# A two-layer Perceiver block on one core: pairs counted while the router runs, stage openings reordered

## The chip, the cores and the metric

The program runs on one core of a Trainium2 chip. The metric is the time of one execution on the device in microseconds (us); less is better. A core has five engines that work side by side and wait for each other through semaphores: TensorE (PE, matrix products; its weight loads are PEld), VectorE (DVE), ScalarE (ACT), GpSimd (POOL) and SyncE (SP, which here only issues transfers).

## What is computed

x is (128 sequences, 32 tokens, 256 numbers), ctx is (128, 257, 256). Every step is added to x; LN is a layer norm without weights.

```python
x0: x += Wo(softmax(q(LN x) . k(ctx) / 4) v(ctx))        # cross-attention, 16 heads of 16, Wq Wk Wv Wo
s0: x += softmax(q(LN x) . k(LN x) / 4) v(LN x)          # self-attention over the 32 tokens
moe: xf = LN(x).reshape(4096, 256)
     routing = softmax(xf @ router_w.T)                  # 8 experts
     top_w, top_i = top_k(routing, 2); top_w /= sum(top_w)
     x += sum over the 2 of top_w * (w_down[e] @ (silu(w_gate[e] @ xf) * (w_up[e] @ xf)))
x1: x += Wo(softmax(q(LN x) . k(ctx) / 4) v(ctx))        # one matrix Wq for q, k and v
s1: x += W_out(causal softmax(rope(q) . rope(k) / 8) v)  # 16 heads of 64, W_qkv is 256 x 3072
bit: x += BitLinear(LN x)
```

## The kernel before

The 4096 tokens are 32 slices (G) of 128 rows; four slices (GPS) make a group, so there are 8 groups (SG). x stays in SBUF as X (128 partitions x 32 slices x 256). The program is five stages, one after the other, each a block with one hand-written list of instructions for each engine: CrossAttention "x0", SelfAndRouter ("s0" and the router, tiles named _moe), Experts ("moe"), CrossAttention "x1", SelfAttention1 ("s1" and "bit"). An engine works through its list in order. Between two stages all five engines meet at a barrier, so nothing of the next stage is issued before the last engine is done with this one.

**s0 and the router.** A loop over g runs one slice of self-attention per step; j is g modulo 4, i is g divided by 4. Group i+1 is prepared in the shadow of group i: its rows are turned at j=0 and projected to q, k, v at j=1, 2, 3 (`project`). The router trails by two groups: at j=0 PE turns the rows of group i-2 (`router.turn`), at j=1 it makes the logits, and DVE makes at j=2 in `choose` some 20 small instructions whose last writes `both`, the table of which 2 of 8 experts each token takes. PE's results go through a ring of only two PSUM banks; who takes a bank waits until it has been emptied (`banks.take(name, signal)`). The loop has 7 steps more than slices, in which the last two groups are routed. SP issues in it the loads of the experts' weights (1.5 MB an expert: 3 experts early, 5 at g=35, `E_FIRST`), the stores of each group's rows (`leave_rows`), and at the end waits for the last of these stores.

**Experts.** 71 tiles of 128 token-expert pairs. First a plan: PE multiplies `both` with a triangle of ones and with ones (`count`), DVE makes running sums over the 32 slices (`scan`), each pair's tile and row (`row`), the experts of the tiles (`plan_experts`), then codes in four pieces (`code`), which PE multiplies; DVE decodes them to token numbers and POOL fetches the rows of a tile with an indirect transfer. SP loads the high halves of the gate and up weights (2 x 4 MB, `fetch_hi`) after the barrier. PE's first product waits for them and for the first tile's rows.

**x1.** A loop over 128 sequences i (j is i modulo 16, a group has 16); DVE takes the maxima of a step's scores (L764), turns v (L780) and the probabilities (L788). At j=5 to 9 the next group of x is normed and turned, at j=12 and 13 projected to q. Before the loop DVE adds the experts' results to group 0 (L844), then norms it. SP keeps one queue of transfers: weights, ctx (1 MB for four sequences), X and y (1.5 MB for a group), and in each step v out to HBM and back to `v_wide`. A load of ctx waits until ctx two groups back has been split into high and low halves.

**s1.** Group 0 is normed (DVE, POOL), turned (PE) and split; the weights Wq, Wk, Wv (1 MB each) are loaded and split by ACT (high) and DVE (low); then slices follow.

A product in high and low halves is three fp32r products (`split_product`, L230). The lines that the steps of the change touch:

```python
sp.wait_ge(self.s.s_pv, "s0", G - 1)           # SelfAndRouter.sync, at g >= G
for e in range(E_FIRST, E):
    self.gates.fetch(sp, self.w.tile, e)
...
dve.wait_ge(self.s.s_x0, i * GPS + GPS - 1)    # take_rows: all four slices
...
for w in (*self.wqkv, self.wout):              # SelfAttention1.sync
    w.load(sp)
```

## Time and profile before

| | us |
|---|---|
| median of 3 runs (2652.72 to 2662.46) | 2653.41 |
| the profiled execution | 2663.03 |
| its span (first to last instruction) | 2661.2 |
| PE busy in the span | 2435.1 (92%) |
| DVE busy | 1827.3 (69%) |
| ACT busy | 1231.6 (46%) |
| POOL busy | 839.3 (32%) |
| mean granted TensorE clock | 0.957 |

The profiled execution is 1.8 us longer than its span and 9.6 us longer than the median of the runs. Busy shares are means over stages that have different limits: in the middle of a stage an engine is nearly full, at the four seams between stages PE is idle or at half clock. The granted clock is a share of full speed: 1.00 is 2.4 GHz, 0.50 is 1.2 GHz.

### The profile page before, as it was taken

The page shows a single profiled execution, that of the slowest core. Times are in us where ns is not written, and L with a number is a line of the kernel's source. Part 1 is how long each engine was busy: PE and PEld are TensorE (multiplying, and loading weights), DVE is VectorE, ACT ScalarE, POOL GpSimd, SP SyncE. Part 2 cuts the span into 40 slices and gives each one's busy share as a digit, 9 for nine tenths or more (in the row PEclk, how much of TensorE's full clock was granted, in tenths as well). Part 3 has the DMA queues.
Part 4 walks back from the last instruction along what each step waited for, and adds up shares of the span by engine and source line. Part 5 has one row for each costly group of instructions (what it writes and reads, how often), then busy time and mean ns, then how long its engine had stood idle before and what let it go on. Part 6 is the DMA issues. An engine that isn't in the chain of part 4 may idle for free. (4 is left out here: it accounts for less than half of the span.)

```text
span 2661.2 us, 102781 instructions
## 1 busy us (share of the span) xinstructions
PE 2435.1 (92%) x44604; PEld 1996.7 (75%) x44604; DVE 1827.3 (69%) x3898; ACT 1231.6 (46%) x2732; POOL 839.3 (32%) x728
## 2 busy tenths in 40 slices
PE   7999999999978846999995989888997999999997
PEld 6888888888845535888884767767775888888885
DVE  5677677767657664222225888888887888888886
ACT  5666565666535423333324666556664322323322
POOL 3233333332222112433335333343321332332331
PEclk9999999999989867999998999999998999999998
DMA  6444555553313253111116776767674000000000
...
DMA packets 171903, 298.94 MB, mean 112 GB/s; under 512 B 26296, under 2 KB 104252, under 8 KB 161984
## 3 DMA queue, kind: packets, MB, share of 16 engines
...
## 5 line engine op out<-in xcount | busy, mean ns | idle before, releaser
L900 POOL TENSOR_TENSOR ctxT_x_lo<-ctx_in_x,ctxT_x_hi 128x514 fp32r<-128x514 f32 x256 | 307.6, 1202 | 757.0 <-ACT ctxT_x_hi L700 757.0
L721 ACT ACTIVATE prob_x<-ps_score_x,neg_max_x 128x257 f32<-128x257 f32 x1024 | 403.5, 480 | 246.3 <-DVE neg_max_x L764 246.3
L764 DVE TENSOR_REDUCE neg_max_x<-ps_score_x 128x2 f32<-128x514 f32 x512 | 328.7, 683 | 99.3 <-PE ps_score_x L611 98.9
L622 PEld LDWEIGHTS ps_v_x<-v_wide_x,probT_x 128*32 128x32 f32 x18432 | 293.9, 110 | 103.2 <-issue 75.3
L622 PE MATMUL ps_v_x<-v_wide_x,probT_x 128*32 128x68 f32 x18432 | 340.5, 226 | 31.5 <-issue 21.6
L788 DVE STREAM_TRANSPOSE probT_x<-prob_x 128x1152 f32<-128x1152 f32 x256 | 345.9, 1351 | 0.0
L2240 POOL TENSOR_TENSOR rot_s<-turned_s,swapped_s 128x512 f32<-128x512 f32 x128 | 164.4, 1297 | 300.5 <-DVE swapped_s L2164 260.4
L611 PE MATMUL ps_score_x<-kT_x,q_x 32*64 32x257 f32 x4096 | 179.4, 406 | 24.6 <-ACT prob_x L721 21.8
L712 ACT ACTIVATE kT_x<-ps_x,bias_k 128x257 f32<-128x257 f32 x256 | 122.1, 477 | 165.1 <-PE ps_x L230 165.1
L1776 DVE TENSOR_TENSOR hid_moe<-ps_up_moe,silu_moe 128x512 f32<-128x512 f32 x71 | 49.1, 692 | 203.0 <-PE ps_up_moe L230 203.0
L230 PE MATMUL ps_x<-ctxT_x_hi,w_q_x_hi 128*128 128x258 f32 x512 | 163.6, 319 | 15.2 <-POOL ctxT_x_lo L900 15.2
L230 PE MATMUL ps_x<-ctxT_x_hi,w_v_x_hi 128*128 128x258 f32 x512 | 160.1, 313 | 12.8 <-POOL ctxT_x_lo L900 11.6
L230 PE MATMUL ps_s<-w_qkv_s_hi,xT_s_hi 128*128 128x512 f32 x384 | 164.4, 428 | 5.5 <-ACT w_qkv_s_hi L264 2.8
L700 ACT ACTIVATE ctxT_x_hi<-ctx_in_x 128x514 fp32r<-128x514 f32 x256 | 161.7, 632 | 6.8 <-DMA ctx_in_x<-ctx 6.8
L230 PE MATMUL ps_x<-ctxT_x_hi,w_k_x_hi 128*128 128x258 f32 x512 | 158.8, 310 | 1.4 <-DVE v_x L780 1.4
L230 PE MATMUL ps_s<-w_qkv_s_lo,xT_s_hi 128*128 128x512 f32 x384 | 152.5, 397 | 0.0
L230 PE MATMUL ps_s<-w_qkv_s_hi,xT_s_lo 128*128 128x512 f32 x384 | 152.3, 396 | 0.0
L230 PE MATMUL ps_x<-ctxT_x_lo,w_q_x_hi 128*128 128x258 f32 x512 | 149.1, 291 | 2.5 <-issue 2.5
L230 PE MATMUL ps_x<-ctxT_x_hi,w_q_x_lo 128*128 128x258 f32 x512 | 148.9, 291 | 0.0
L2117 ACT ACTIVATE attnT_s_hi<-ps_s 128x512 fp32r<-128x512 f32 x64 | 38.1, 598 | 232.4 <-PE ps_s L2035 232.4
L230 PE MATMUL ps_x<-ctxT_x_lo,w_v_x_hi 128*128 128x258 f32 x512 | 145.4, 284 | 0.0
L230 PE MATMUL ps_x<-ctxT_x_hi,w_k_x_lo 128*128 128x258 f32 x512 | 145.3, 284 | 0.0
...
## 6 DMA issues: line engine op xcount, KB each, us to landing
...
v_wide_x<-v_x SPq DMA_DIRECT2D x512, 76.5 KB, 2.2
v_out_x<-v_x SPq DMA_DIRECT2D x128, 306.0 KB, 3.2
v_wide_x<-v_out_x SPq DMA_DIRECT2D x512, 76.5 KB, 2.6
...
```

The lines of the kernel that those rows point to most:

```text
L230: last = pe.do.matmul(out, a, b, start=n == 0, stop=n == len(steps) - 1)
L611: ins = pe.do.matmul(self.ps[m * 2 * T:(m + 1) * 2 * T, r, 0:S], q, self.kT[b % 3][rows, m, 0:S], start=True, stop=True)
L622: ins = pe.do.matmul(self.ps_v[r * T:(r + 1) * T, b % 2, :, :], self.probT[b % 3][:, r, n * T:(n + 1) * T], self.v_wide[b % 4][:, :, r, n, ...
L700: act.do.activation(self.ctxT[b % 3].hi[:, :, 0:S], self.ctx_in[g % 2][:, :, j, :], ACT.Copy).then_inc(*s.ctx_hi.at(tag, b))
L712: act.do.activation(out, src, ACT.Identity, bias=self.biases["k"][:, m:m + 1]).then_inc(*s.k.at(tag, b, m))
L721: act.do.activation(self.prob[b % 3][:, r, 0:S], self.ps[:, r, 0:S], ACT.Exp, bias=self.neg_max[b % 2][:, r:r + 1]).then_inc(*s.exp.at(tag ...
L764: dve.do.tensor_reduce(self.neg_max[b % 2][:, r], self.ps[:, r, 0:S], AX_X, ALU.max, negate=True).then_inc(*s.neg_max.at(tag, b, half))
L788: dve.do.transpose(flat(self.probT[b % 3]), flat(self.prob[b % 3])).then_inc(*s.prob_T.at(tag, b))
L900: pool.do.tensor_tensor(self.ctxT[b % 3].lo[:, :, 0:S], self.ctx_in[g % 2][:, :, j, :], self.ctxT[b % 3].hi[:, :, 0:S].bitcast(F32), ALU.s ...
L1776: dve.do.tensor_tensor(self.hid[t % 2][:, :], self.up_ps[t % 2][:, :], self.silu[t % 2][:, :], ALU.mult).then_inc(*s.hid.at(t))
L2117: act.do.activation(self.attnT.hi[:, c * 512:(c + 1) * 512], banks["attn", g, c][:, :], ACT.Copy).then_inc(*s.a_hi.at(g, c))
L2240: pool.do.tensor_tensor(self.rot[e][:, :, :], self.turned[e][:, :, :], self.swapped[e][:, :, :], ALU.add).then_inc(*s.r_rot.at(g, i, c))
```

## The change

Four parts.

1. **Counting moves into s0.** The new class Places counts a group's pairs as soon as the group is routed: five bf16 products of 128 x 40 on PE (`count`, at j=3, from the same ring of two banks) and two DVE instructions (`add`). `both` becomes bf16 with five empty slices beside each group's four, so that the five products give running sums. The two big products, the scan of 32 slices and its memsets go from Experts; `plan_experts` moves behind the four codings; the memsets of x_in move from DVE to POOL.
2. **Loads and the last rows.** Experts 5 to 7 are loaded after the last rows have been stored (`E_SECOND`). `take_rows` waits slice by slice; in the last steps ACT scales the last rows before the exponent of the group ahead, not after it.
3. **x1's opening.** X and y of group 0 are loaded first; DVE splits the low half of the weight after it has added y, not before.
4. **s1's opening moves into x1.** Group 0 of x is normed, turned and split during x1's last 16 steps (stats at j=5, 6, scale at 7, halves at 8, 9). Wq is loaded at i=112 and split in steps 126 to 129, into tiles that the ctx halves have left; Wk and Wv are loaded after the last ctx has been split.

```diff
 class Places:
+    def count(self, pe, i, banks):
+        bank, emptied = banks.take(("count", i), self.s.plan, "placed", i)
+        pe.wait_ge(self.s.route, i, ROUTE_STEPS - 1)
+        if emptied:
+            pe.wait_ge(*emptied)
+        out = bank[:, 0:(GPS + 1) * E]
+        for d in range(GPS + 1):
+            ins = pe.do.matmul(out, (self.ones if d else self.below)[:, :],
+                               self.both[:, i, GPS - d:2 * GPS + 1 - d, :].rearrange("p g e -> p (g e)"), start=d == 0, stop=d == GPS)
+        ins.then_inc(*self.s.counted.at(i))
+    def add(self, dve, i, banks):
+        ...
+            dve.do.tensor_tensor(self.place[:, g, :], out[:, 0:GPS, :], self.total[:, i - 1, :].unsqueeze(1).to_broadcast([P, GPS, E]),
+                                 ALU.add)
+            dve.do.tensor_tensor(self.total[:, i, :], out[:, GPS, :], self.total[:, i - 1, :], ALU.add).then_inc(*s.plan.at("placed", i))
 SelfAndRouter.sync:
-                    for e in range(E_FIRST, E):
+                    for e in range(E_FIRST, E_SECOND):
                         self.gates.fetch(sp, self.w.tile, e)
...
+        for e in range(E_SECOND, E):
+            self.gates.fetch(sp, self.w.tile, e)
 SelfAndRouter.tensor:
             if now is not None:
                 a.scores(pe, g)
+            if j == 3 and routed is not None:
+                self.places.count(pe, routed, banks)
...
+        self.places.count(pe, SG - 1, banks)
 SelfAndRouter.scalar:
+            if g == G + 1:
+                router.scale(act, rows)
             if j == 1 and routed is not None:
                 router.exponent(act, routed)
-            if g == G + 1:
-                router.scale(act, rows)
 SelfAndRouter.vector:
         def take_rows(i):
-            dve.wait_ge(self.s.s_x0, i * GPS + GPS - 1)
             for n in range(GPS):
+                dve.wait_ge(self.s.s_x0, i * GPS + n)
                 router.ln.take_stats(dve, i, n)
...
             if now is not None:
                 a.find_max(dve, g)
+            if j == 3 and routed is not None:
+                self.places.add(dve, routed, banks)
 Experts.vector:
         plan()
-        plan_experts()
         dve.wait_ge(s.plan, "row")
         for c in range(2 * G // CHUNK):
             code(c)
+        plan_experts()
 CrossAttention.sync:
+        if self.opening:
+            load_y(0)
         for n in self.of_ctx:
             self.w[n].load(sp)
         load_ctx(0)
...
+            if self.opening and i == B - BPS:
+                sp.wait_ge(s.y_added, SG - 1)
+                self.opening.wq.load(sp)
...
+        if self.opening:
+            sp.wait_ge(s.ctx_hi, tag, B - 1)
+            sp.wait_ge(s.ctx_lo, tag, B - 1)
+            for w in self.opening.wkv:
+                w.load(sp)
 CrossAttention.vector:
+            if self.opening and n == SG:
+                if j in (5, 6):
+                    dve.wait_ge(s.x_out, tag, GPS - 1)
+                    for half in range(GPS // 2):
+                        self.opening.ln.take_stats(dve, 0, (j - 5) * (GPS // 2) + half)
+                if j == 7:
+                    self.opening.ln.scale(dve, 0)
+                if j in (8, 9):
+                    dve.wait_ge(s.q_ps, tag, SG - 1, KD - 1)
+                    self.opening.ln.keep_lo(dve, 0, j - 8, banks)
+            if self.opening and 0 <= i - B < 2:
+                dve.wait_ge(s.k_ps, tag, B - 1, KD - 1)
+                self.opening.wq.split_lo(dve, i - B)
 SelfAttention1.vector:
-        for j in range(GPS):
-            self.ln.take_stats(dve, 0, j)
-        self.ln.scale(dve, 0)
-        self.wqkv[0].split_lo(dve)
-        prepare(0)
         self.wqkv[1].split_lo(dve)
```

What the lists of the engines look like at three places. Names carry the stage (_s0, _moe, _x1, _s1); in brackets are the signals that an instruction waits for.

PE at a step j=3 of s0 before: scores of the slice (q_s0 and kT_s0), then the two halves of v of the next group (w_v_s0), then the weighing of the slice ahead (probT).

```order
L1153 MATMUL ps_score_s0<-kT0_s0,q0_s0_15937 64x32 [waits s_shift]
L1153 MATMUL ps_score_s0<-kT0_s0,q0_s0_15937 64x32 x31
L1114 MATMUL ps_1_s0<-xT1_s0,w_v_s0 128x512 [waits k]
L1114 MATMUL ps_1_s0<-xT1_s0,w_v_s0 128x512
L1114 MATMUL ps_0_s0<-xT1_s0,w_v_s0 128x512 [waits k]
L1114 MATMUL ps_0_s0<-xT1_s0,w_v_s0 128x512
L1193 MATMUL ps_v0_s0<-v_wide0_s0_15941,probT0_s0 32x68 [waits s_out,s_probT]
L1193 MATMUL ps_v0_s0<-v_wide0_s0_15941,probT0_s0 32x68 x15
L1153 MATMUL ps_score_s0<-kT1_s0,q1_s0_15938 64x32 [waits s_shift]
```

And in the change:

```order
L1210 MATMUL ps_score_s0<-kT0_s0,q0_s0_15937 64x32 [waits s_shift]
L1210 MATMUL ps_score_s0<-kT0_s0,q0_s0_15937 64x32 x31
L1403 MATMUL ps_1_s0<-both_routed,below_placed 128x40 [waits k,route]
L1403 MATMUL ps_1_s0<-both_routed,ones_placed 128x40 x4
L1171 MATMUL ps_0_s0<-xT1_s0,w_v_s0 128x512 [waits k]
L1171 MATMUL ps_0_s0<-xT1_s0,w_v_s0 128x512
L1171 MATMUL ps_1_s0<-xT1_s0,w_v_s0 128x512 [waits plan]
L1171 MATMUL ps_1_s0<-xT1_s0,w_v_s0 128x512
L1250 MATMUL ps_v0_s0<-v_wide0_s0_15941,probT0_s0 32x68 [waits s_out,s_probT]
```

The count stands ahead of the v products and waits for the route, which is DVE's `choose`; the second half of v takes the bank of the count, and so waits for "plan", which is DVE's `add` of this step.

PE at the end of s0 and over the barrier before: logits of group 6, turns of the last rows (group 7), its logits, then the two products that count all pairs.

```order
L1263 MATMUL ps_0_s0<-router_moe,xT0_moe 128x8 [waits m_xT]
L1263 MATMUL ps_0_s0<-router_moe,xT0_moe 128x8 x7
L349 MATMUL ps_1_s0<-constants,ln_xn1_moe 128x128 [waits ln_moe_xn]
L349 MATMUL ps_1_s0<-constants,ln_xn1_moe 128x128 x3
L349 MATMUL ps_0_s0<-constants,ln_xn1_moe 128x128 [waits route]
L349 MATMUL ps_0_s0<-constants,ln_xn1_moe 128x128 x3
L1263 MATMUL ps_1_s0<-router_moe,xT1_moe 128x8 [waits m_xT]
L1263 MATMUL ps_1_s0<-router_moe,xT1_moe 128x8 x7
L2282 UNCONDITIONAL_BRANCH
L2283 UNCONDITIONAL_BRANCH [waits barrier_Pool_Activation_PE_DVE_SP_release]
L1535 MATMUL ps_0_moe<-both_routed,constants 128x256 [waits route]
```

And in the change:

```order
L1320 MATMUL ps_0_s0<-router_moe,xT0_moe 128x8 [waits m_xT]
L1320 MATMUL ps_0_s0<-router_moe,xT0_moe 128x8 x7
L1403 MATMUL ps_1_s0<-both_routed,below_placed 128x40 [waits route]
L1403 MATMUL ps_1_s0<-both_routed,ones_placed 128x40 x4
L352 MATMUL ps_0_s0<-constants,ln_xn1_moe 128x128 [waits ln_moe_xn]
L352 MATMUL ps_0_s0<-constants,ln_xn1_moe 128x128 x3
L352 MATMUL ps_1_s0<-constants,ln_xn1_moe 128x128 [waits plan]
L352 MATMUL ps_1_s0<-constants,ln_xn1_moe 128x128 x3
L1320 MATMUL ps_0_s0<-router_moe,xT1_moe 128x8 [waits m_xT]
L1320 MATMUL ps_0_s0<-router_moe,xT1_moe 128x8 x7
L1403 MATMUL ps_1_s0<-both_routed,below_placed 128x40 [waits route]
```

The count of group 6 now stands between the logits of group 6 and the turns of group 7, and the count of group 7 ahead of the barrier.

DVE in x1 before: from a turn of probabilities (L788) at i=117 into the next step, and the end of the stage with the first row of s1.

```order
L788 STREAM_TRANSPOSE probT2_x1<-prob2_x1 128x1152 [waits exp]
L811 COPY attn0_x1<-ps_2_x1 128x4x32 [waits weighed_T]
L764 TENSOR_REDUCE neg_max0_x1<-ps_score_x1 128x2 [waits score]
L764 TENSOR_REDUCE neg_max0_x1<-ps_score_x1 128x2
L780 STREAM_TRANSPOSE v2_x1<-kT2_x1 128x9x2x16 [waits k,v_left0]
L780 STREAM_TRANSPOSE v2_x1<-kT2_x1 128x9x2x16 [waits k]
...
L811 COPY attn1_x1<-ps_0_x1 128x4x32 [waits weighed_T]
L815 TENSOR_TENSOR X<-X,ps_1_x1 128x256 [waits o_ps]
L815 TENSOR_TENSOR X<-X,ps_2_x1 128x256
L2282 UNCONDITIONAL_BRANCH
L2303 UNCONDITIONAL_BRANCH [waits barrier_Pool_Activation_PE_DVE_SP_release]
L302 BN_STATS ln_stats_s1<-X 128x6
```

And in the change:

```order
L827 STREAM_TRANSPOSE probT2_x1<-prob2_x1 128x1152 [waits exp]
L305 BN_STATS ln_stats_s1<-X 128x6 [waits x_out]
L307 BN_AGGR ln_mean_var_s1<-ln_stats_s1 128x2 [waits ln_stats]
L305 BN_STATS ln_stats_s1<-X 128x6
L307 BN_AGGR ln_mean_var_s1<-ln_stats_s1 128x2 [waits ln_stats]
L850 COPY attn0_x1<-ps_2_x1 128x4x32 [waits weighed_T]
...
L827 STREAM_TRANSPOSE probT1_x1<-prob1_x1 128x1152 [waits exp]
L274 TENSOR_TENSOR split<-loaded,split 128x1024 [waits w_hi,w_in_s1_qkv0,k_ps]
L274 TENSOR_TENSOR split<-loaded,split 128x1024 [waits w_hi]
...
L2359 UNCONDITIONAL_BRANCH
L2380 UNCONDITIONAL_BRANCH [waits barrier_Pool_Activation_PE_DVE_SP_release]
L274 TENSOR_TENSOR w_qkv1_s1_lo<-loaded,w_qkv1_s1_hi 128x1024 [waits w_hi,w_in_s1_qkv1]
```

Statistics of s1's group 0 have moved from behind the barrier into the last 16 steps, and the low halves of Wq (split<-loaded,split) to just behind the last turn of probabilities; s1 begins with the low half of Wk.

## Rows read from the trace of the kernel before

**Rows 1.** The page's first line.

```profile
span 2661.2 us, 102781 instructions
```

**Rows 2.** Timeline of a step j=3 in s0: start us, us, engine, line, what.

```profile
908.79 3.70 PE L1114 MATMUL ps_s<-xT_s,w_v_s 128*128 128x512 f32 x8
...
909.90 0.18 DVE L1312 TENSOR_TENSOR both_routed<-hot_routed 128x32 f32<-128x32 f32 x1
...
911.94 0.69 DVE L1166 TENSOR_TENSOR shifted_s<-ps_score_s,neg_max_s 128x512 f32<-128x512 f32 x1
...
912.42 0.52 PEld L1193 LDWEIGHTS ps_v_s<-v_wide_s,probT_s 128*32 128x32 f32 x32 [0.76 <-issue]
...
914.96 0.68 DVE L1162 TENSOR_REDUCE neg_max_s<-ps_score_s 128x16 f32<-128x512 f32 x1
```

**Rows 3.** Timeline of the last steps of s0 and the router.

```profile
969.84 2.07 ACT L340 ACTIVATE ln_xn_moe<-X,ln_shift_moe,ln_rstd_moe 128x256 f32<-128x256 f32 x4 [0.33 <-POOL ln_shift_moe L322]
...
971.85 0.19 DVE L1312 TENSOR_TENSOR both_routed<-hot_routed 128x32 f32<-128x32 f32 x1
971.96 1.56 PEld L349 LDWEIGHTS ps_s<-constants,ln_xn_moe 128*128 128x128 f32 x8 [3.27 <-ACT ln_xn_moe L340]
...
981.25 0.18 DVE L1312 TENSOR_TENSOR both_routed<-hot_routed 128x32 f32<-128x32 f32 x1
```

**Rows 4.** SP's longest waits at that seam: us, times, longest.

```profile
SPq L80 <- DMA xn_out<-ln_xn_moe: 18.5, 1, 18.5
```

**Rows 5.** Timeline from the barrier to the experts' first tile.

```profile
992.40 0.43 SPq L431 DMA_DIRECT2D X<-up_hi_out  x1
...
997.32 0.16 DVE L1677 TENSOR_SCALAR ends_moe<-scan_moe 128x8 f32<-128x8 f32 x1
...
1000.90 0.73 DVE L1708 TENSOR_TENSOR passed_moe<-constants,ends_moe 1x568 f32<-1x568 f32 x1
...
1002.65 1.32 DVE L1723 TENSOR_TENSOR tile_hot_moe<-numbers_moe,tile_moe 128x1136 bf16<-128x1136 bf16 x1
...
1025.52 0.66 PE L1558 MATMUL ps_moe<-constants,x_in_moe 128*128 128x128 f32 x2 [5.12 <-DMA x_in_moe<-xn_out,from_token_moe]
```

**Rows 6.** Transfers of 940 to 1060 us: KB each, median us from issue to landing.

```profile
X<-up_hi_out SPq DMA_DIRECT2D x1, 4096.0 KB, 21.3
```

**Rows 7.** Timeline of x1's opening.

```profile
1405.17 0.33 SPq L257 DMA_DIRECT2D w_in_q_x<-x_q  x1
...
1410.70 1.16 ACT L700 ACTIVATE ctxT_x_hi<-ctx_in_x 128x514 fp32r<-128x514 f32 x2 [2.25 <-DMA ctx_in_x<-ctx]
...
1414.89 0.55 PE L230 MATMUL ps_x<-ctxT_x_hi,w_q_x_hi 128*128 128x258 f32 x1 [15.19 <-POOL ctxT_x_lo L900]
1415.01 4.20 DVE L844 SCALAR_TENSOR_TENSOR X<-y_in_x,share_routed,X 128x256 f32<-128x256 f32 x8 [5.76 <-DMA y_in_x<-y_out]
...
1424.27 0.93 PEld L349 LDWEIGHTS ps_x<-constants,ln_xn_x 128*128 128x128 f32 x5 [4.18 <-DVE ln_xn_x L330]
```

**Rows 8.** Windows there and in s0: busy of PE, PEld, DVE, ACT, POOL; PEclk, DMA share, GB/s.

```profile
1421.00:1424.00 3.00, 0.00 (x0) 0.00 (x0) 2.52 (x9) 0.00 (x0) 1.05 (x1) 0.96 1.00 352
1424.00:1427.00 3.00, 1.97 (x8) 1.57 (x8) 0.93 (x3) 1.32 (x3) 0.00 (x0) 0.50 0.69 243
1427.00:1430.00 3.00, 2.23 (x5) 1.82 (x6) 0.67 (x1) 0.40 (x1) 1.10 (x1) 0.50 0.00 0
...
896.00:902.00 6.00, 6.00 (x19) 3.04 (x18) 4.53 (x17) 2.12 (x4) 0.58 (x1) 0.72 0.00 0
```

**Rows 9.** Timeline of x1: maxima (L764) of i=101, 106, 117 and 122.

```profile
1910.84 1.29 DVE L764 TENSOR_REDUCE neg_max_x<-ps_score_x 128x2 f32<-128x514 f32 x2
...
1936.18 1.28 DVE L764 TENSOR_REDUCE neg_max_x<-ps_score_x 128x2 f32<-128x514 f32 x2
...
1983.97 1.29 DVE L764 TENSOR_REDUCE neg_max_x<-ps_score_x 128x2 f32<-128x514 f32 x2
...
2001.60 1.29 DVE L764 TENSOR_REDUCE neg_max_x<-ps_score_x 128x2 f32<-128x514 f32 x2
```

**Rows 10.** Timeline of s1's opening: its first row and PE's first product.

```profile
2036.11 0.43 DVE L302 BATCH_NORM_STATS2 ln_stats_s<-X 128x6 f32<-128x256 f32 x1 [0.32 <-PEq L2282]
...
2045.83 0.77 PE L230 MATMUL ps_s<-w_qkv_s_hi,xT_s_hi 128*128 128x512 f32 x1 [2.77 <-ACT w_qkv_s_hi L264]
```

204 lines of the change are left out of this document (116 added, 88 removed).

## The prediction

> **What bounds the kernel now.** I read the page's first line for the span [rows 1], then the windows, to see which engine is full in each stage, then the waits at the seams, and last the timelines around each place that the change touches. In s0 PE is the full engine: over six us it is busy for all six [rows 8]. In x1 PE and DVE take turns; where a step has only its own work, DVE's maxima and transposes set its length. At the seams nobody is full: one chain of small steps and transfers runs alone. So an instruction added in s0 costs what it holds PE up, one added in x1's light steps costs its DVE time, and one removed from a seam gives back its whole length.
>
> **Seam from s0 to the experts.** Before, the last `both` ends at 981.4 [rows 3], but SP waits 18.5 us for the store of the last rows [rows 4], which is queued behind five experts' loads, and the next block begins at 992.0, with its first transfer at 992.40 [rows 5]. In the change only two experts (3 MB) stand ahead of that store, and the other three are issued behind it. At 394 GB/s (the two high-half loads, 8.4 MB in 21.3 us [rows 6]) the 4.7 MB that are no longer ahead of it are 12 us, so it lands near 980. The engines' own chain sets the end now. Taking slices one by one and scaling before the exponent brings the last scale forward by 0.85 us; but the exponent of group 6 then runs behind it (2.07 us), so `choose` of group 6 ends at about 973.9 where it was 972.0, PE counts it, and only then turns the last rows, at 974.7 instead of 971.96 [rows 3]: 2.8 late. From turn to last `both` is as before 9.3 us (984.0), then come the last count and add (1.5, estimated from five short products and two DVE instructions of 0.2 with a hand-over at each) and the barrier (0.5): the next block starts at 986.0, not 992.0. That is 6.0.
>
> Behind the barrier 4.9 us of memsets, two big products and scan (992.40 to 997.32) become about 0.4, the last codes no longer stand behind `plan_experts` (1000.90 to 1002.65, 1.75) [rows 5], and the rest of the way to the first turn of rows stays. 1025.52 minus 6.0, 4.9 and 1.75, plus 0.15 for what is left, gives 1013.0: 12.5 sooner. The high halves must be there too. They landed at 1013.7, 21.3 us after their issue [rows 5, 6]; the queue ahead of them holds the same bytes as before and drains at 990, so they land at 1010 to 1012, 1 to 3 us before they are wanted. Gain **12.5**, bounds 9 (the load ends last) and 15 (chain of the last rows not delayed).
>
> Here a page bears on the size. The rows give 8.4 MB in 21.3 us, 394 GB/s. The Trainium skill, "DMA: Bandwidth & Descriptors", section "Where 436 GB/s comes from", puts HBM to SBUF at about 358 GB/s a core. By that alone the two loads would take 23.4 us, land at 1013.5 and cost half a us of this gain; the trace does not agree, and its rate is the one used.
>
> **Counting in s0.** At a step j=3 PE does scores, then eight v products (3.70, so 1.85 a half), which start at 908.79 and end at 912.49 [rows 2]. The count stands ahead of them and waits for `both`, which ends at 910.08 [rows 2]. Queued behind it on PE are the v products, the weighing and the next scores, for which DVE and ACT wait. The count itself is small (five products of 40 columns in bf16, at most 0.4), the first half ends at 912.4; the second takes the count's bank, and so waits for DVE's add, which stands behind `shifted` (ends 912.63) and is done by 913.1: it ends at 914.95, 2.5 late. The next maxima come at 917.0 instead of 914.96, 2.0 to 2.1 late, as a little slack lies between. Of the seven counts in the loop the first five (groups 0 to 4) meet a projection; the next meets none and costs nothing, and the one of group 6 is in the seam above. Loss 5 x 2.05 = **10**. Bounds: 7 (1.4 each, the wait for `both` alone with no wait for the add) and 20 (4.1 each, below). DVE's two additions of 0.2 a group lie in DVE's idle time.
>
> **x1's opening.** Before, ctx landed for 1410.70 and y for 1415.01, and the maxima of the chain are y's additions (4.20), norm, and the turn at 1424.27 [rows 7]. The loads are issued from 1405.17; 1.25 MB arrive by 1410.70 and 1.5 MB more in the 4.3 after, 352 GB/s [rows 7, 8]. With y first it lands at about 1411.5, 3.5 sooner, and ctx at 1415.1, 4.4 later. The additions then end at 1415.7 rather than 1419.2; but PE's first product, 1414.89 [rows 7], waits for ctx and its split until 1417.1. PE's nine products of this ctx fill 1417.1 to 1422.4, so the turn comes at 1422.4 (not 1420.8): 1.85 sooner. Then the clock: before the turn PE had been idle from 1421 to 1424, and from 1424 to 1430 its 4.20 us of work ran at 0.50 [rows 8], that is at 1.2 GHz. With no such idle time it stays at 2.4 GHz; half of 4.20 is 2.1, of which I take 1.65, as part waits for other engines. Together **+3.5** gained, bounds 1.8 (clock falls all the same) and 4.
>
> The page to weigh is the Trainium skill, "TensorE: Matmul & The Clock Gate", section "HAM oscillation — how this bites in real kernels": short idle times between bursts of products can drop the array to half clock. By it both the gain here and a danger in s0 would follow: each count puts two idle times into PE's full stretch. The trace has 0.72 granted in a stretch where PE is busy throughout [rows 8], so here the clock can be low without idle time at all.
>
> **s1's opening, moved into x1.** Before, the stage begins at 2036.1 and PE's first product stands at 2045.83 [rows 10]. With turned rows and Wq split, it comes within some tenths of the barrier: +9.6. Three prices. First, statistics, scaling and low halves now lie in x1's last 16 steps. The trace prices this: five steps with another group's norm took 1936.18 - 1910.84 = 25.34, five without 2001.60 - 1983.97 = 17.63, so **7.7** [rows 9]; those were heavier by a store and y's addition on POOL, so 7.3 (5 to 9, below: DVE's added busy time alone). Second, Wq (1 MB) goes on SP's queue at i=112, just ahead of the ctx load at 113, with no y load beside it; earlier bursts of 1.5 MB cost between 0.2 and 6.3 each: 1.5 (0 to 4). Third, the splits of Wq at the very end lie in ACT's and DVE's idle time while the last probabilities are weighed: 0 (1.5 if DVE is late with them). Wk's and Wv's loads are awaited behind the first slice's q, so nothing. Net 9.6 - 7.3 - 1.5 = **+0.8**, bounds -4 and +4.
>
> **Sum.** 12.5 - 10 + 3.5 + 0.8 = 6.8, say 7 sooner. The profiled execution took 2663.03 (span 2661.2 [rows 1] and 1.8 around it), so 2656.0; the median of the runs is 9.6 below that execution: 2646.4, and I say **2646**.
>
> **Rivals.**
> - *Counts are absorbed.* If `both` comes sooner against PE (the sixth count and the light steps show slack) or the delay of one step is made up in the next, where DVE's and ACT's work waits on hand-overs, the loss falls from 10 to 2. For it: a group's cycle has other small idle times; against it: PE is full in the loop, and what is pushed on a full engine is not made up. Gain 15, time **2638**. Chance 0.22.
> - *The seam's gain is held by a transfer.* The indirect fetch of the first rows used to run with the queue empty; now it is issued during the last us of the 8.4 MB and may land only behind them, 1013.7 plus the fetch's own time [rows 6]; with its 5 us of wait [rows 5] the first turn is at 1019: the seam gives 6.5, not 12.5. Gain 1, time **2652**. Chance 0.13.
> - *Slower.* The counts' idle times in s0 double their price: either the low clock (in [rows 8] at 0.72 in the middle of s0) falls further after each, or the transposed v comes too late for the store and its reload. One row's arithmetic: the v half that waits, at half clock, is 3.7 and not 1.85. At 4.1 a step the loss is 20.5 and the whole 3.7 slower, **2657**. It decides the sign from a step's price of 3.4 on (16.8 / 5), and passes 0.5% at 6. Chance 0.12.
> - The forecast itself, 0.53.
>
> **How the numbers follow.** A difference of 0.5% (13.3 us) is about what a measurement of this kernel can tell from none. Faster than that is most of the first rival (0.85 of 0.22) and an eighth of the forecast (several terms at their good ends): 0.25. Slower by that much takes a third of the slow rival and a little of the rest: 0.05. The rest is 0.70. The range 2634 to 2658 holds the first rival's time with 4 us to spare and the slow one's; the likeliest case alone spans 2640 to 2653.
>
> **What would show it.** SP's longest wait at the seam under 3 us; the block behind it starting 6 us sooner in the same count; the first turn of expert rows 12 to 13 sooner, ahead of it the landing of the high halves by 1 to 3; in s0 maxima of a step after j=3 some 2 us later than a step with no count, five times; in x1 the turn at 1422 with a clock above 0.9 in the six us after; five steps with statistics taking 25 where they took 17.6; s1's first product within 1 us of its beginning. The prediction is wrong if the v products' second half waits for something else than the add, or if x1's last steps, which I price by steps in mid-stage, hide the norm.

## The result

| | before | changed |
|---|---|---|
| median (8 runs each, taken together) | 2653.6 us | 2640.09 us |
| lowest to highest | 2650.03 to 2674.04 | 2632.95 to 2645.56 |
| ratio, 95% interval | | 0.9925 (0.9899 to 0.9952) |
| a second, later measurement (17 and 6 runs) | | 0.9926 (0.9905 to 0.9947) |

The ratio times the median shown ahead, 2653.41, is 2633.5 us: half a us under the predicted range, and 20 us of gain where 7 were forecast. The means of the two measurements give 17.6 and 17.8 us, the two medians above 13.5; all are about twice the forecast or more. The case held to be likeliest (within 0.5%) did not occur.

The page of the changed kernel begins so (span; then busy time, share, instructions of each engine):

```profile
span 2633.6 us, 102876 instructions
PE 2428.3 (92%) x44640; PEld 1989.7 (76%) x44640; DVE 1818.9 (69%) x3904; ACT 1230.1 (47%) x2732; POOL 839.8 (32%) x732
```

The span is 27.6 us shorter than that of [rows 1], more than the kernels differ: executions of the kernel before lie up to 24 us apart, those of the change 13, and these two lay 5.9 above and 4.1 below the mean of theirs. PE's busy time is 6.8 us less than the 2435.1 of before, so most of the gain is idle time taken away.

**s0, a step j=3.** The timeline of the changed kernel that answers to [rows 2] (start us, us, engine, line, what; in brackets the idle time before it and what ended it):

```profile
913.57 0.19 PE L1403 MATMUL ps_s<-both_routed,below_placed 128*128 128x40 bf16 x1 [1.29 <-DVE both_routed L1369]
913.71 1.96 PE L1171 MATMUL ps_s<-xT_s,w_v_s 128*128 128x512 f32 x4
...
914.65 0.68 DVE L1219 TENSOR_REDUCE neg_max_s<-ps_score_s 128x16 f32<-128x512 f32 x1
915.36 0.69 DVE L1223 TENSOR_TENSOR shifted_s<-ps_score_s,neg_max_s 128x512 f32<-128x512 f32 x1
915.97 0.18 DVE L1413 TENSOR_TENSOR place_placed<-ps_s,total_placed 128x32 f32<-128x32 f32 x1
916.07 0.16 DVE L1415 TENSOR_TENSOR total_placed<-ps_s,total_placed 128x8 f32<-128x8 f32 x1
...
916.28 1.98 PE L1171 MATMUL ps_s<-xT_s,w_v_s 128*128 128x512 f32 x4 [0.61 <-DVE total_placed L1415]
...
920.13 0.68 DVE L1219 TENSOR_REDUCE neg_max_s<-ps_score_s 128x16 f32<-128x512 f32 x1
```

This is the mechanism that was forecast, each step of it: the count waits 1.29 for `both`, the first half of v follows, the second waits 0.61 for DVE's add, which stands behind `shifted`. From one step's maxima to the next it takes 5.48 us; in [rows 2], where `shifted` starts 0.71 behind its maxima, it was 914.96 - 911.23 = 3.73. So a count costs this step 1.75, not 2.05.

**The seam.** The last rows, the barrier and the way to the first expert rows, for [rows 3] and [rows 5]; behind them SP's longest wait at the seam ([rows 4]; under 3 was forecast) and the high halves' transfer ([rows 6]):

```profile
973.70 2.07 ACT L343 ACTIVATE ln_xn_moe<-X,ln_shift_moe,ln_rstd_moe 128x256 f32<-128x256 f32 x4 [2.11 <-POOL ln_shift_moe L325]
...
978.23 0.18 DVE L1369 TENSOR_TENSOR both_routed<-hot_routed 128x32 bf16<-128x32 f32 x1
978.65 1.95 PE L352 MATMUL ps_s<-constants,ln_xn_moe 128*128 128x128 f32 x8
...
987.93 0.19 DVE L1369 TENSOR_TENSOR both_routed<-hot_routed 128x32 bf16<-128x32 f32 x1
...
989.48 0.43 SPq L434 DMA_DIRECT2D X<-up_hi_out  x1
...
993.38 1.34 DVE L1810 TENSOR_TENSOR tile_hot_moe<-numbers_moe,tile_moe 128x1136 bf16<-128x1136 bf16 x1
...
1013.14 1.25 POOL L1877 DMA_INDIRECT x_in_moe<-xn_out,from_token_moe  x1 [22.84 <-issue]
...
1017.17 0.66 PE L1655 MATMUL ps_moe<-constants,x_in_moe 128*128 128x128 f32 x2 [6.03 <-DMA x_in_moe<-xn_out,from_token_moe]
```
```profile
SPq L80 <- DMA xn_out<-ln_xn_moe: 4.0, 1, 4.0
```
```profile
X<-up_hi_out SPq DMA_DIRECT2D x1, 4096.0 KB, 27.2
```

And the fetch of the first expert rows before, for [rows 5]:

```profile
1022.33 1.25 POOL L1795 DMA_INDIRECT x_in_moe<-xn_out,from_token_moe  x1 [52.59 <-DVE to_pair_moe L1744]
```

The engines' chain now sets the end of s0: PE turns the last rows at 978.65, behind the count of group 6, 9.3 us later the last `both` begins, and SP's first transfer behind the barrier comes 1.6 us after that. From that table to the first turn of expert rows there are 29.2 us where there were 44.3. The high halves landed 27.2 us after their issue, at 1016.7 and not at 1010 to 1012; PE's first product of the experts came at 1018.95, so PE did not wait for them, but the cover was 2 us. The fetch of the first rows did take a little longer beside them: 4.03 us from its issue to the turn (1013.14 to 1017.17), where it had been 3.19 (1022.33 to 1025.52).

**x1's opening** (for [rows 7, 8]; the windows' columns are those of [rows 8]):

```profile
1396.74 0.32 SPq L548 DMA_DIRECT2D X<-x_left  x1
...
1403.69 3.38 DVE L884 SCALAR_TENSOR_TENSOR X<-loaded,share_routed,X 128x256 f32<-128x256 f32 x8 [5.59 <-DMA loaded<-y_out]
...
1409.02 0.77 PE L230 MATMUL ps_x<-split,w_q_x_hi 128*128 128x258 f32 x2 [17.75 <-POOL split L955]
...
1414.20 1.09 PE L352 MATMUL ps_x<-constants,ln_xn_x 128*128 128x128 f32 x8 [0.79 <-DVE ln_xn_x L333]
```
```profile
1414.00:1417.00 3.00, 1.11 (x9) 0.91 (x9) 1.43 (x3) 1.61 (x3) 0.42 (x1) 1.00 0.26 96
1417.00:1420.00 3.00, 3.00 (x12) 2.12 (x12) 0.00 (x0) 1.26 (x2) 0.68 (x1) 1.00 0.00 0
```

The additions of y start 6.95 us behind the first load (9.84 before), the turn 17.46 (19.10 before), and the clock is at 1.00 for q where it was at 0.50: from the first load to the first maxima 25.4 us, before 29.1.

**s1's opening.** The end of x1 and the first product of s1, for [rows 10]:

```profile
2002.83 0.91 SPq L256 DMA_DIRECT2D loaded<-s_qkv  x2
2003.44 2.32 DVE L274 TENSOR_TENSOR split<-loaded,split 128x1024 fp32r<-128x1024 f32 x2
...
2008.17 0.97 PE L653 MATMUL ps_v_x<-v_wide_x,probT_x 128*32 128x68 f32 x49 [2.29 <-issue]
...
2010.62 3.79 PE L674 MATMUL ps_x<-w_o_x,attn_x 64*128 64x256 f32 x16 [0.38 <-DVE attn_x L850]
...
2015.68 1.19 PE L230 MATMUL ps_s<-split,xT_first_hi 128*128 128x512 f32 x2 [1.27 <-PEq L2359]
```

PE's first product comes 13.5 us after the last turn of probabilities at 2002.15; before it was 21.1 (2024.75 to 2045.83). That is 7.5 of the 9.6 forecast. The product does come at once when the block begins (SP's first row of it is at 2015.48); but the block begins 13.3 us behind that last turn, where it was 11.4 (2024.75 to 2036.11). PE stops for 2.29 us within a run of equal products, with nothing that the profile shows to wait for ("issue"), while the loads of Wk and Wv, which begin at 2002.83, are under way.

**Where the rest came from.** A step in x1's loop far from any edit, before (group 3, i=51), and its like in the change:

```profile
1671.05 1.34 DVE L788 STREAM_TRANSPOSE probT_x<-prob_x 128x1152 f32<-128x1152 f32 x1
1671.86 0.56 PE L622 MATMUL ps_v_x<-v_wide_x,probT_x 128*32 128x68 f32 x24 [2.20 <-issue]
...
1676.29 1.29 DVE L764 TENSOR_REDUCE neg_max_x<-ps_score_x 128x2 f32<-128x514 f32 x2 [0.87 <-PE ps_score_x L611]
```
```profile
1672.00:1675.00 3.00, 3.00 (x37) 2.60 (x32) 0.39 (x1) 0.47 (x2) 0.00 (x0) 0.65 0.38 91
```
```profile
1654.36 1.29 DVE L803 TENSOR_REDUCE neg_max_x<-ps_score_x 128x2 f32<-128x514 f32 x2
...
1655.37 0.80 PE L653 MATMUL ps_v_x<-v_wide_x,probT_x 128*32 128x68 f32 x36 [0.39 <-issue]
```

Before, PE stops 2.20 us in the middle of the 72 products of a step, its clock stands at 0.65 in the three us behind that (it had been 1.00), and the next maxima are late; in the change the stop at this place is 0.39. Such stops of over 0.7 us between equal products (taken from the start of one weight load to the start of the next, which adds some 0.1 to 0.2 to the idle time) are 24.8 us in sum in the first trace of before (12 of them, up to the seventh group's end) and 17.5 in that of the change (10). Where they stand is told with the experiments.

### The profile page after: what moved, and what is told of

The parts are those of the page before. It is cut to its first block and busy times, and to the rows that moved or that the text cites. A ratio compares the mean times of both kernels' runs of the same rounds, so it can differ in the third digit from the quotient of the medians.

```text
span 2633.6 us, 102876 instructions
## 1 busy us (share of the span) xinstructions
PE 2428.3 (92%) x44640; PEld 1989.7 (76%) x44640; DVE 1818.9 (69%) x3904; ACT 1230.1 (47%) x2732; POOL 839.8 (32%) x732
## 3 DMA queue, kind: packets, MB, share of 16 engines
q8 instruction: 356, 5.83, 0.9%
## 5 line engine op out<-in xcount | busy, mean ns | idle before, releaser
L653 PEld LDWEIGHTS ps_v_x<-v_wide_x,probT_x 128*32 128x32 f32 x18432 | 288.3, 109 | 100.9 <-issue 71.7
L653 PE MATMUL ps_v_x<-v_wide_x,probT_x 128*32 128x68 f32 x18432 | 335.1, 224 | 30.9 <-issue 21.8
L955 POOL TENSOR_TENSOR ctxT_x_lo<-ctx_in_x,ctxT_x_hi 128x514 fp32r<-128x514 f32 x128 | 154.5, 1208 | 417.2 <-ACT ctxT_x_hi L733 417.2
L955 POOL TENSOR_TENSOR split<-loaded,split 128x514 fp32r<-128x514 f32 x128 | 153.2, 1197 | 323.6 <-ACT split L733 323.6
L230 PE MATMUL ps_x<-split,w_q_x_hi 128*128 128x258 f32 x1024 | 209.6, 302 | 19.9 <-POOL split L955 17.7
L230 PEld LDWEIGHTS ps_x<-split,w_q_x_hi 128*128 128x128 f32 x1024 | 162.4, 196 | 34.1 <-ACT split L733 18.5
L230 PE MATMUL ps_x<-split,w_q_x_lo 128*128 128x258 f32 x512 | 148.1, 289 | 0.0
L230 PE MATMUL ps_x<-ctxT_x_hi,w_v_x_lo 128*128 128x258 f32 x512 | 144.9, 283 | 0.0
L230 PEld LDWEIGHTS ps_x<-ctxT_x_hi,w_v_x_hi 128*128 128x128 f32 x512 | 97.2, 190 | 63.0 <-issue 48.3
L230 PE MATMUL ps_x<-ctxT_x_lo,w_k_x_hi 128*128 128x258 f32 x512 | 144.6, 282 | 0.0
```

What stands on the lines that cost most here:

```text
L230: last = pe.do.matmul(out, a, b, start=n == 0, stop=n == len(steps) - 1)
L653: ins = pe.do.matmul(self.ps_v[r * T:(r + 1) * T, b % 2, :, :], self.probT[b % 3][:, r, n * T:(n + 1) * T], self.v_wide[b % 4][:, :, r, n, ...
L955: pool.do.tensor_tensor(self.ctxT[b % 3].lo[:, :, 0:S], self.ctx_in[g % 2][:, :, j, :], self.ctxT[b % 3].hi[:, :, 0:S].bitcast(F32), ALU.s ...
```

## The experiments

A kernel's traces are cut at landmarks: **s0** from its first maxima to its last (32 slices), **end** from there to the last `both`, **seam** to the first turn of expert rows, **experts** to x1's first maxima (the opening of x1 is in it), **loop** to the 113th turn of probabilities (the seven groups that no edit touches), **tail** to the last one, **to s1** to s1's first maxima. "Ratio" is to the kernel before, timed beside it on the same chip. "Dev" says how far the profiled execution lay from the mean of its kernel's runs.

| | s0 | end | seam | experts | loop | tail | to s1 | dev | ratio (interval) |
|---|---|---|---|---|---|---|---|---|---|
| before, first trace | 182.5 | 21.7 | 44.3 | 408.7 | 534.2 | 56.3 | 48.7 | +5.9 | 1 |
| before_again | 181.2 | 22.9 | 43.2 | 409.2 | 530.1 | 55.8 | 46.4 | -2.3 | (one run) |
| tiles_only | 185.8 | 22.9 | 43.1 | 409.0 | 523.0 | 55.9 | 48.3 | -2.8 | 1.0002 (0.9988 to 1.0017) |
| y_first | 184.4 | 22.9 | 43.3 | 405.6 | 526.4 | 57.6 | 48.5 | +0.7 | 0.9991 (0.9981 to 1.0002) |
| before_pad | 182.2 | 21.7 | 45.2 | 409.6 | 517.9 | 59.2 | 46.0 | -5.6 | 0.9994 (0.9977 to 1.0011) |
| before_pad65 | 184.1 | 22.9 | 56.1 | 409.4 | 521.2 | 56.0 | 45.9 | -6.1 | 1.005 (1.0031 to 1.0069) |
| parts_12 | 186.9 | 23.6 | 29.2 | 410.0 | 520.1 | 57.7 | 47.5 | -7.6 | 0.997 (0.995 to 0.9989) |
| parts_123 | 190.4 | 23.6 | 29.7 | 405.1 | 521.8 | 59.7 | 49.2 | +1.2 | 0.9949 (0.9929 to 0.9969) |
| opening_in_s1 | 189.5 | 23.6 | 29.0 | 404.8 | 517.1 | 59.0 | 46.1 | -5.0 | 0.9932 (0.9915 to 0.995) |
| y_later | 192.6 | 23.6 | 29.3 | 409.8 | 519.0 | 68.5 | 40.4 | +3.5 | 0.9964 (0.995 to 0.9979) |
| change, first trace | 188.3 | 23.6 | 29.2 | 405.0 | 514.0 | 66.0 | 41.8 | -4.1 | 0.9925 (0.9899 to 0.9952) |
| after_again | 192.6 | 23.6 | 29.8 | 405.2 | 526.1 | 65.2 | 40.7 | +7.3 | 0.9926 (0.9905 to 0.9947) |
| after_pad | 188.2 | 23.6 | 29.3 | 405.0 | 526.6 | 67.1 | 41.9 | +7.1 | 0.9939 (0.9919 to 0.9959) |
| after_pad130 | 189.1 | 23.6 | 29.2 | 404.9 | 526.7 | 66.7 | 42.0 | +5.8 | 0.9961 (0.9946 to 0.9977) |
| after_pad218 | 185.2 | 23.6 | 29.4 | 404.9 | 525.7 | 62.3 | 38.9 | -5.7 | 0.9943 (0.9924 to 0.9961) |
| after_pad44 | 189.3 | 23.6 | 29.4 | 405.2 | 524.5 | 63.3 | 37.1 | +7.0 | 0.9931 (0.9911 to 0.995) |
| loads_ahead | 188.1 | 23.6 | 37.2 | 405.3 | 514.1 | 64.9 | 41.2 | -8.8 | 0.997 (0.9955 to 0.9985) |
| count_late | 181.5 | 23.7 | 29.2 | 405.6 | 515.2 | 66.3 | 40.2 | -5.2 | 0.9911 (0.9895 to 0.9927) |
| late_exponent | 183.1 | 23.8 | 28.4 | 407.4 | 516.9 | 64.6 | 43.0 | +3.8 | 0.9897 (0.9876 to 0.9918) |
| late_exponent_pad | 182.0 | 22.2 | 31.0 | 405.6 | 519.3 | 65.5 | 42.9 | -0.3 | 0.9927 (0.9901 to 0.9953) |

Between traces that share the edit, end, seam and experts agree within 3 us, so they price the edits there; s0 lies within 8, tail and the way to s1 within 7, and the loop within 17.

### Does the surplus repeat, and is it part 4?

before_again and after_again are the two kernels unchanged.

> The kernel before, unchanged, for a second trace of it. The first traces differ by 27.6 us, 18.3 of them in x1's loop ahead of the last group of 16 steps, where the change adds and removes no instruction; they lie in a few steps behind the issue of a load of y (i mod 16 of 2 to 7). Theory 'chance' (how the transfers of ctx, y and v fall together varies from one execution to the next): the loop from the first maxima to the end of the seventh group of 16 takes another number here, lower than in the first trace by 5 us or more, since that execution was 9.6 above the median; the steps that are long are other ones. Theory 'order' (the change makes the transfers fall better each time): within 3 us of the first trace, the same steps long.

> The changed kernel, unchanged, for a second trace and a narrower interval. Chance: x1's loop ahead of the last group within 10 us of its first trace on either side and other steps long. Order: it stays some 18 us under the kernel before. Both: ratio 0.990 to 0.995, first expert rows turned 13 us sooner than the loop of s0 alone would have them, s0's loop 6 us longer.

> The change with its part 4 undone in work (norm, turn and split of s1's first group, loads of Wq, Wk, Wv and Wq's split are all done in s1 again; the shared tiles stay). The prediction's price: gain of 9.6 at s1's opening against 7.3 and 1.5 in x1, so this kernel is 1 us slower than the change, within 5. Rival: part 4 carries much of the measured gain, since the first product of s1 comes sooner and x1's last steps hide the norm: this kernel is 6 us or more slower. In the trace: x1's last 16 steps shorter than the change's by 7 us, or by under 3.

```diff
-            if self.opening and i == B - BPS:
-                sp.wait_ge(s.y_added, SG - 1)
-                self.opening.wq.load(sp)
...
-            if self.opening and n == SG and j in (8, 9):
-                self.opening.ln.turn(pe, 0, j - 8, banks)
...
 SelfAttention1.sync:
-        self.wout.load(sp)
+        for w in (*self.wqkv, self.wout):
+            w.load(sp)
```

(the same on ACT, DVE and POOL; the loads of Wk and Wv leave x1 too; neither is shown)

> The kernel before with part 3 of the change alone: X and y of group 0 are loaded ahead of Wq and ctx, and the low half of Wq is split behind y's addition. The prediction says 3.5 us sooner at x1's first maxima, and nothing else: ratio 0.9987. Theory 'order': the moved loads also shift how later loads fall, and the loop is shorter by 10 us or more: ratio 0.995. Chance: the loop's length lies anywhere within 10 us of the kernel before.

The edit of y_first, in the opening's list of loads (and `split_lo` behind y's addition):

```diff
+        if self.y_in:
+            load_y(0)
         for n in self.of_ctx:
             self.w[n].load(sp)
         load_ctx(0)
...
-        if self.y_in:
-            load_y(0)
```

Before's loop took 530.1, 4.1 less than the first time, between what the two theories said; the change's took 526.1, 12 more than the first time, beyond even what "chance" allowed. Between the second traces 4 us are left of the first ones' 20. The whole kernels' ratio did repeat. Part 4 undone (0.9932) is as fast as the change (0.9926): not the carrier. Part 3 gave 3.3 in the stage where it was expected (408.9 in the mean of before's two traces, now 405.6) and 2.7 us in the means of the whole, where the interval of the ratio still includes 1.

### The place in PE's code

In both kernels the stops within equal products fall at positions in PE's list (counted in the records of its weight-load side: the loads and the waits between them) that are whole multiples of 129.4 apart:

```
first trace of before, nine of its 12: position (step of the loop, stop in us)
23648 (19, 1.42)  23907 (21, 2.51)  25330 (35, 2.72)  27012 (51, 2.43)  28694 (67, 2.50)
28952 (69, 3.43)  30376 (83, 2.67)  30764 (86, 1.44)  32445 (101, 2.54)
first trace of the change, six of its 10
23650 (19, 1.86)  25332 (35, 2.28)  29084 (69, 1.43)  29601 (75, 2.61)  30766 (85, 2.76)
31283 (90, 1.28)
differences: 1682 = 13.0 x 129.4, 259 = 2.0 x, 3752 = 29.0 x, 1165 = 9.0 x
```

The pages also count transfers of instructions on a queue of their own: 356 packets, 5.83 MB, 16 KB each. The traces hold the times of each packet, and they settle what a stop is: all 234 stops of over 0.7 us in the loops of the twenty traces end 1.0 to 1.7 us after one of these packets has landed, though they land only some 5.7 us apart. So at a stop PE waits for a piece of its code. The packet itself takes about 1 us, as those do that nobody waits for, so it is its start that is late. Other transfers alone do not explain that, since s1 has a few such stops (of 0.7 to 2.0 us) with the DMA engines nearly idle. In before, a window (columns as above: the last three are granted clock, DMA share, GB/s) and the loads in it:

```profile
2222.00:2232.00 10.00, 8.87 (x169) 7.38 (x168) 7.89 (x18) 2.18 (x4) 5.10 (x4) 1.00 0.01 2
```
```profile
2228.53 1.13 PEld L978 LDWEIGHTS ps_score_s<-kT_s,qT_s 64*32 64x32 f32 x123 [0.17 <-issue]
2230.91 0.14 PEld L978 LDWEIGHTS ps_score_s<-kT_s,qT_s 64*32 64x32 f32 x5 [1.25 <-issue]
```

What delays the packet was not tested. The change, with 41 more such records (36 of them loads) on PE ahead of x1, moves each piece's border to another place in a step. Added idle products at the beginning of the experts move it with little other effect (before_pad's seam is 1.7 longer):

```diff
         count()
+        for _ in range(20):
+            pe.do.matmul(self.gate_ps[0][:, 0:8], self.consts["ident"][:, :], self.consts["ident"][:, 0:8], start=True, stop=True)
         code()
```

> The kernel before with 20 small products more on PE (128x8, f32, into a bank that nobody reads before its next write) at the beginning of the experts, where PE waits for DVE anyway. They do no work; they move all of PE's later instructions by as many places in its code as the change does (some 41 in the count of weight loads). Theory 'code': in x1's loop PE stops for 0.7 to 3.4 us in the middle of equal products, always at instruction numbers that are a multiple of 129.4 apart, so a piece of its code arrives late behind the transfers; which step that hits depends on the place of the instructions, and the change moves it. Then the loop ahead of its last group is 514 to 526 us here (530 to 534 before), with stops of 15 to 20 us in sum (25 to 30 before), and the whole is 8 to 11 us sooner: ratio 0.996. Theory 'transfers' (the change's own moved loads and tiles shorten the loop): the loop stays 530 to 534, ratio 1.000.

> The changed kernel with 88 small products more on PE (128x8, bf16, into an unread bank) at the same place, so that x1's instructions stand where the kernel before has them within a piece of code of 129.4. Code: x1's loop ahead of its last group goes back to 526 to 534 us, stops of 25 to 30 in sum, ratio to the kernel before 0.9965 instead of 0.9926. Transfers: the loop stays 514 to 526, ratio 0.993. Should the 88 products outlast PE's wait for the codes, that costs a us at the first expert rows.

```diff
+        for _ in range(88):
+            pe.do.matmul(self.gate_ps[0][:, 0:8], self.places.ones[:, :], self.places.ones[:, 0:8], start=True, stop=True)
         code()
```

The places moved as said: of before_pad's 12 stops six stand where the change has them (steps 19, 35, 69, 75, 85, 90), and after_pad has 15 stops and 25.4 us. The loops came out as the theory had them, too (517.9 and 526.6). But before_pad's stops were still 23.9 us in sum, where 15 to 20 were expected, and the time did not follow in the size expected: 0.9994 and not 0.996, 0.9939 and not 0.9965. Three more places were tried:

> The changed kernel with 130 small products more at the beginning of the experts: one whole piece of PE's code (129.4 of the recorded loads), so x1's products stand in their pieces where the change has them. Code: x1's loop ahead of its last group as in the nine traces with that place (514 to 526, mean 518), stops of PE in it of 12 to 24 us in sum, ratio 0.992 to 0.994. Theory 'any shift' (the added products themselves lengthen something): as with 88 more, loop 526 and ratio 0.9939 or more.

> The same with 218 more (88 and a whole piece): x1's products stand where the kernel before has them. Code: loop as in the five traces with that place (523 to 534, mean 528), ratio 0.995 to 0.997. Chance (single traces only looked different): the loop and the ratio are those of the change, 518 and 0.993.

> The same with 44 more: a place that no run has had, a third of a piece further. Code: the loop takes a length of its own, anywhere between 510 and 540, with its stops in other steps than either. Chance: 518 to 522, ratio 0.993.

The change's own place, one whole piece further, came out as the slowest of the padded ones (0.9961) with the fewest stops (8, 17.6 us); before's place gave 0.9943 with 17 stops and 30.6 us. So the place decides at which steps PE stops, but not the time: the theory "code" is refuted as the cause of the surplus (what the change gained beyond the stages with edits). before_pad65 made the other control:

> The kernel before with 65 small f32 products more at the beginning of the experts: one piece of PE's code, so x1's products stand in their pieces as in the kernel before. Theory 'place': as before, ratio 1.000 plus the time of the 65 products (1 to 3 us in front of the first codes), 1.001. Theory 'every build has its own offset' (the change with 130 more, which should have been as the change, was 9 us slower): anything from 0.997 to 1.003, with a loop of its own.

(the loop of before_pad with `range(65)`; the padded changes have `range(130)`, `range(218)`, `range(44)`)

Its 65 f32 products, each recorded as two, outlast PE's wait for the codes (timeline):

```profile
995.99 27.74 PE L1606 MATMUL ps_gate_moe<-constants 128*128 128x8 f32 x130
```

They were expected to cost 1 to 3 us. The seam is 12.6 longer than the 43.5 of the unpadded kernels (56.1), the mean of the runs 13.5 longer: the rest of the kernel is within 1 us of before, as "place" has it.

### Tiles and parts

> The kernel before with only the tiles of part 4: ctx, y, the halves of ctx and s1's stages share the two big tiles of the change; no instruction, load or wait is moved. With the runs so far corrected for how far each profiled execution lay from its kernel's median, x1's loop ahead of its last group is some 528 us in the kernels with before's tiles (the padded one too) and 521 with the change's tiles (the padded one too). Theory 'tiles': the loop is 521 here too, ratio 0.9975. Theory 'code' (the place of PE's instructions in pieces of code): nothing changes, ratio 1.000, loop 526 to 534. Theory 'before x1' (the surplus lies ahead of x1 and only looks like x1's in single traces): ratio 1.000.

```diff
-        self.ctx_in = [sb(f"ctx_in{i}", [P, KD, BPG, S]) for i in range(2)]
+        self.ctx_in = opening.ctx_in if opening else [sb(f"ctx_in{i}", [P, KD, BPG, S]) for i in range(2)]
...
-        self.y_in = sb("y_in", [P, 2, GPS, D]) if y_out is not None else None
+        self.y_in = opening.y_in if opening else None
```

> Parts 1 and 2 alone: counting in s0, the loads and last rows; x1 and s1 with the lists and tiles of before. From the stages of the traces so far: s0's loop 6 to 8 longer, its end 1 to 2 longer, from the last table of experts to the first expert rows 14.5 shorter: 6 us sooner in all, ratio 0.9977 if x1's loop is as before. Code (PE's x1 instructions moved by 41 places as in the change): x1's loop shorter as well, ratio 0.994 to 0.995. Tiles: 0.9977.

> Parts 1, 2 and 3 with before's tiles, s1's opening in s1: differs from the kernel with part 4 undone (ratio 0.9932) by the tiles alone. Tiles: 6 to 7 us slower than that, ratio 0.9958. Code: the same, 0.993.

> The change with its part 3 undone: y of group 0 is loaded behind Wq and ctx, and Wq's low half is split ahead of y's addition, as before. Theory 'y first' (the order of the opening also moves how the later loads of ctx, y and v fall in x1's loop): kernels with y first have loops of 521 us in the mean, corrected for how far each profiled execution lay from its kernel's mean, the others 528; so undoing it costs 3.5 at the opening and 6 in the loop, ratio 0.996. Theory 'opening only': 3.5 us, ratio 0.994.

y_later undoes the diff of y_first in the change; parts_12 and parts_123 put x1's and s1's lists and tiles back, with and without that diff; tiles_only gives the kernel before the two big tiles alone. Tiles alone change nothing (1.0002). The means of the runs give 9.7 us for parts 1 and 2, 14.4 with part 3, 17.6 to 18.6 with part 4's tiles, with or without its work; between parts_123 and opening_in_s1, which differ by the tiles alone, the intervals overlap. y_later is 8 us slower than the change; 4.6 of them are at the opening (409.8 against 405.2).

### The two disputed prices in front of x1

> The changed kernel with the count of a group behind the v products and the weighing of its step, and DVE's add behind its transposes there. By the prediction's reason (PE held by the wait for both and by the bank of the count) s0's loop, 188 to 193 us in the change and 181 to 184 before, is back under 186: ratio 0.990 to 0.991. Rival: the count costs wherever it stands, as PE's clock in this stretch is what is lost: the loop stays at 188 or more, ratio 0.9926. The instructions after s0 keep their places in PE's code.

```diff
             if now is not None:
                 a.scores(pe, g)
-            if j == 3 and routed is not None:
-                self.places.count(pe, routed, banks)
...
             if 1 <= g < G:
                 a.weigh(pe, g - 1)
+            if j == 3 and routed is not None:
+                self.places.count(pe, routed, banks)
```

(and DVE's `add` behind `turn_prob`). Its timeline at a step j=3:

```profile
912.03 3.70 PE L1171 MATMUL ps_s<-xT_s,w_v_s 128*128 128x512 f32 x8
...
913.14 0.18 DVE L1369 TENSOR_TENSOR both_routed<-hot_routed 128x32 bf16<-128x32 f32 x1
...
916.64 0.18 PE L1403 MATMUL ps_s<-both_routed,below_placed 128*128 128x40 bf16 x1 [0.29 <-DVE v_s L1197]
```

The eight v products run through in 3.70, the count finds `both` long done, and s0 takes 181.5: the loss is gone to the last us, the whole is 7 us faster than the change by the means. The rival, that the clock is what is lost, fails with it; the granted clock of s0 is 0.88 to 0.92 in all traces, with the early count, the late one or none.

> The changed kernel with all five late experts' loads ahead of the store of the last rows again, and none behind it. The prediction's price: SP's wait for that store is the end of the stage again, some 15 us long, and the experts' block begins 6 us later than the last counts allow; ratio 0.9948. Rival (the chain of the last rows has become so long that the store is back in time): within 2 us of the change, 0.993.

```diff
-E_FIRST, E_SECOND = 3, 5
+E_FIRST, E_SECOND = 3, 8
```

```profile
SPq L80 <- DMA xn_out<-ln_xn_moe: 19.1, 1, 19.1
```

SP waits 19.1 us for the last rows' store again ([rows 4]) and the seam is 8.0 longer (37.2 against 29.2); the means differ by 8.7. That is more than half of what end and seam gain together (13.0).

> The changed kernel with the late count (ratio 0.9911 by itself) and, besides, the exponent of the group ahead done before the scale of the last rows again, as in the kernel before. The prediction put the exponent's place at 2.1 us of the end of s0 and the sooner scale at 0.85: by it the end of s0 (last maxima to last table, 23.7 us with the late count) is about 22.5 and the kernel is 1 us faster, ratio 0.9907. Rival: the scale then waits for the exponent, and the last rows come later by as much as that gains: no change within 0.5 us.

```diff
-            if g == G + 1:
-                router.scale(act, rows)
             if j == 1 and routed is not None:
                 router.exponent(act, routed)
+            if g == G + 1:
+                router.scale(act, rows)
```

> The version with the late count and the exponent ahead (ratio 0.9897) with 130 small products more at the beginning of the experts. Does its lead over the change hold in another build? Stages in front of x1 say 7 us for the late count and 0 to 1 for the exponent: against the change with 130 more (0.9961) it should be 7 us faster, 0.9935; if the late count's gain was luck of the build, 0.996.

End and seam together take 52.2 and 53.2, with the late count alone 52.9: the exponent's place does nothing, as the rival said. The late count is the version that beats both kernels: 0.9911 and 0.9897 against 0.9926 in one build, 0.9927 against 0.9961 in the other. The intervals overlap in each of these pairs, but the sign is the same three times, and the stage s0 shows 6 to 8 us in every trace (181.5 to 183.1 against 189.1 in the mean).

## Why the prediction was wrong

- **Seam, 12.5 forecast.** End and seam went from 22.5 + 43.5 to 23.6 + 29.4 in the means: 13.0. Right in size. The split within it was off. The end grew by 1.1 and not by 2.6, as the exponent's place costs nothing (late_exponent). In the first traces the block behind the barrier begins 25.1 us behind the last maxima where it was 32.9, so 7.7 sooner and not 6.0; what follows it is 5.4 shorter (27.7, before 33.1) and not 6.5. Of the 1.1 that are missing there 0.8 is the rival of the held transfer, in small: the high halves landed 5 us later than forecast, and the fetch beside them took 4.03 for 3.19. The order of the loads by itself is worth 8 (loads_ahead).
- **"Loss 5 x 2.05 = 10".** Right in mechanism, too large: s0 went from 183.4 (six traces without a count) to 189.1 (eleven with the early one): 5.7. In the first trace of the change the steps j=3 take 5.48, one of them 6.30, where they took 3.74. But the two steps behind each of the first four sum to 57.4, where the same eight took 60.8 in the first trace of before: part of what is late is made up there, and the sum had no term for that. The term was 4 us too dear, and the rival of the absorbed counts (2 in place of 10) was about half right.
- **x1's opening, 3.5.** 4.1 (409.4 to 405.3 in the means of the stage). Right, the clock's share included.
- **s1's opening, 9.6 - 7.3 - 1.5 = 0.8.** The last group costs 8.0 (57.5 to 65.5, from 56.3 to 66.0 in the first traces), against 8.8; five steps with s1's statistics take 24.0 for 17.6. The way to s1 is 6.5 shorter (47.4 to 40.9), against 9.6. Net -1.5, and undoing the work changed nothing. The mis-sized term is the gain at the opening: "Wk's and Wv's loads are awaited behind the first slice's q, so nothing" left out that they run while PE still works on x1. In PE's last weighing there a stop is 2.7 to 4.5 us long in nine of the eleven traces with these loads; in the nine without them it is 0.8 to 2.0, or missing. The other two, after_pad218 and after_pad44, have the border of the piece elsewhere and no such stop: tail and way to s1 take 101.3 and 100.4 together, where the nine take 105.9 to 109.0 and the kernels without part 4 104.8 in the mean. So where PE does not stop, part 4 gains 4 in these two stages. (Neither of the two builds was faster as a whole.)
- **The step that failed most: x1's loop at nothing.** The stages with edits sum to 13.0 - 5.7 + 4.1 - 1.5 = 9.9, 3 more than forecast. The measured means are 17.6 and 17.8; so some 8 us come from stages where nothing was moved. The sum put all of these at nothing, without a reason. The first traces showed 20 in the loop; 10 and more of it was which executions had been profiled.

What is shown of those 8: not the tiles (1.0002), not the place in the code as such (five places, no order), not part 4's work. The same lists built with idle products elsewhere spread from 0.9926 to 0.9961, 9 us, though the intervals of these two just touch: a build may have an offset of several us. The mean of the change and its four padded builds is 15.2 us under before, so some 2 of the 8 are luck of this build.

The rest goes with parts 1 and 2 more clearly than with anything else. Take from each kernel's gain (in the means of the runs) what its edited stages give: the four variants of before without parts 1 and 2 keep -1.4, -0.9, -0.2 and 4.3 us, the thirteen with them 0.5 to 11.2, 5.6 in the mean. The loops say the same once each trace is corrected by its "dev": 527.2 in the mean of the six without, 520.6 in the fourteen with, with single ones on the wrong side (parts_12 527.7, after_pad218 531). Part 3's order, which "y first" held for the cause, parts them less well (525.8 and 520.8; y_first 525.7, y_later 515.5). This grouping was found behind the runs and tested by none, and no edit of parts 1 and 2 lies in x1: why its loop, some 5 us or 0.2%, is shorter behind them stays open. The two signs that the prediction named for being wrong did not come up: the second half of v waits for the add, and x1's last steps do not hide the norm. PE's wait for its code, which no term or bound held, lengthens both kernels.
